# Setup and the first pass of a GNN chain in one block, fourteen sets of one-hot rows with a signal per seven blocks, and running sums in PSUM

## What is computed

```python
edge_index = jnp.stack([src, dst])
x = _layernorm(x + _L0_gnn_ref(x, edge_index, L0_gnn_W1, L0_gnn_b1, L0_gnn_W2, L0_gnn_b2), axis=-1)
x = _layernorm(x + _L1_gnn_ref(x, edge_index, edge_attr_16, L1_gnn_Wf, L1_gnn_bf, L1_gnn_Ws, L1_gnn_bs, ...), axis=-1)
x = _layernorm(x + _L2_gnn_ref(x, edge_index, edge_attr_16, L2_gnn_W, L2_gnn_W_edge, ...), axis=-1)
x = _layernorm(x + _L3_gnn_ref(x, edge_index, batch0, L3_gnn_W1, L3_gnn_b1, ..., L3_gnn_Wf, L3_gnn_bf), axis=-1)
```

```python
def gcn_layer(x, src, dst, W, b, n_nodes):
    h = x @ W
    deg = jax.ops.segment_sum(jnp.ones(src.shape[0], x.dtype), dst, num_segments=n_nodes) + 1.0
    dis = jax.lax.rsqrt(deg)
    norm = dis[src] * dis[dst]
    msg = h[src] * norm[:, None]
    agg = jax.ops.segment_sum(msg, dst, num_segments=n_nodes)
    agg = agg + h * (dis * dis)[:, None]
    return agg + b
```

## Time and profile before

| | us |
|---|---|
| median of 3 runs | 12125.48 |
| lowest, highest | 12105.85, 12148.87 |
| profiled execution, own time | 12032.11 |
| its span | 12030.4 |

### The profile page before, as it was taken

One profiled execution on the slowest core, in us unless ns is written; L12 is line 12 of the kernel. 1 busy time (PEld: TensorE's weight loads), 2 busy tenths in 40 slices (PEclk: granted clock), 3 DMA queues, 4 the chain that ended last, 5 costly groups with the idle time before them and its releaser, 6 DMA issues. The chain is left out here.

```text
span 12030.4 us, 142319 instructions
## 1 busy us (share of the span) xinstructions
PE 6638.5 (55%) x32436; PEld 5450.5 (45%) x32436; DVE 8099.9 (67%) x33889; ACT 5912.3 (49%) x13869; POOL 7313.3 (61%) x6801
## 2 busy tenths in 40 slices
PE   2140666665666466677746666674455465553333
PEld 1020665654555466667745565673233343332221
DVE  2063778995666799989988888444556566764444
ACT  0000445775766799989957776231123332322222
POOL 5700446886777688866636665555654565556665
PEclk6575888887878655568867877555567655665555
DMA  3338777884222477744424444453334333332221
GB/s 95 94 105 268 241 240 253 289 290 154 72 71 71 140 234 236 234 134 142 142 87 160 165 163 146 128 143 84 85 111 129 105 102 90 119 97 56 56 56 52
DMA packets 1019501, 1694.48 MB, mean 141 GB/s; under 512 B 304877, under 2 KB 535080, under 8 KB 1018594
## 3 DMA queue, kind: packets, MB, share of 16 engines
q1 hardware_dynamic: 782752, 1361.06, 33.9%
q0 software_dynamic: 175936, 218.82, 8.4%
q10 hardware_dynamic: 59970, 105.49, 2.7%
HBM read 988.03 MB, written 707.78 MB: 141 GB/s over the span
## 5 line engine op out<-in xcount | busy, mean ns | idle before, releaser
L1319 POOL DMA_INDIRECT g_got<-scaled,row_src x2352 | 2225.1, 946 | 1567.3 <-issue 681.3
L589 PE MATMUL g_a_p_z<-sb_L_gnn_W,g_a_u_t 128*128 128x128 f32 (+3 forms) x2574 | 653.3, 398 | 986.2 <-ACT g_a_u_t L1164 368.0
L881 DVE SCALAR_TENSOR_TENSOR g_sums<-g_got,first,g_sums 128x128 f32<-128x128 f32 (+3 forms) x3136 | 864.2, 276 | 373.6 <-DMA g_got<-scaled,row_src 117.3
L589 PEld LDWEIGHTS g_a_p_z<-sb_L_gnn_W,g_a_u_t 128*128 128x128 f32 (+1 forms) x2574 | 485.0, 267 | 1158.1 <-issue 555.0
L885 DVE SCALAR_TENSOR_TENSOR g_sums<-g_sums,cont,g_got 128x128 f32<-128x128 f32 (+3 forms) x3128 | 880.1, 281 | 125.7 <-DVE g_sums L881 73.1
L1319 POOL DMA_INDIRECT g_got<-xs,idx_src x392 | 369.8, 943 | 926.7 <-POOLq L175 551.1
L1164 ACT COPY g_a_u_t<-g_a_p_t 128x512 f32<-128x512 f32 (+3 forms) x495 | 225.0, 455 | 1393.3 <-remote 762.0
L589 PE MATMUL g_bb_p_z<-sb_L_gnn_W,g_bb_u_t 128*128 128x128 f32 (+2 forms) x4302 | 834.5, 362 | 117.8 <-DVE g_bb_z L1056 76.2
L589 PEld LDWEIGHTS g_bb_p_z<-sb_L_gnn_W,g_bb_u_t 128*128 128x128 f32 x4302 | 754.2, 261 | 165.8 <-issue 137.1
L1164 ACT COPY g_bb_u_t<-g_bb_p_t 128x1024 f32<-128x1024 f32 (+2 forms) x294 | 233.6, 795 | 1123.0 <-PE g_bb_p_t L580 623.7
L1231 POOL DMA_INDIRECT out<-g_a_o,idx_out x396 | 394.5, 996 | 363.1 <-ACT g_a_o L641 250.7
(11 more groups left out here) (495 smaller groups left out, 23885.1 us busy)
## 6 DMA issues: line engine op xcount, KB each, us to landing
raw<-gb_u SPq DMA_DIRECT2D x98, 768.0 KB
xs<-f_o ACTq DMA_DIRECT2D x97, 516.0 KB
f_x<-in_x ACTq DMA_DIRECT2D x97, 512.0 KB
g_bb_own<-in_x SPq DMA_DIRECT2D x97, 512.0 KB
wide<-g_bb_o SPq DMA_DIRECT2D x97, 512.0 KB
g_bb_own<-wide SPq DMA_DIRECT2D x97, 512.0 KB
g_bb_res<-in_x SPq DMA_DIRECT2D x97, 512.0 KB
x<-g_bb_o SPq DMA_DIRECT2D x97, 512.0 KB
```

The lines of the kernel that those rows point to most:

```text
L589: last = nc.tensor.matmul(dst_psum[0:p, q * g * width:(q * g + n) * width], turned_tile[0:n * k, q * P:q * P + p], weight[0:n * k, 0:n * w ...
L881: nc.vector.scalar_tensor_tensor(out=self.firsts, in0=new, scalar=first[:, col], in1=self.firsts, op0=ALU.mult, op1=ALU.add).then_inc(run_ ...
L1319: pool.indirect_dma_start(got[b.s4][:, c * row:(c + 1) * row], None, table, bass.IndirectOffsetOnAxis(ap=index[:, b.n * CH + c:b.n * CH + ...
```

## The change

Three edits, with new constants HOT = 14 and COUNTED = 7.

1. Setup's Block and its barrier are gone; its instructions stand in the first pass's Block. POOL: all constants, then a wait on the new semaphore dst_ready, then the gathers. SP: all loads, then the stores of gathered rows, then gate_wa's stores. ACT: the weight loads, then as before, with setup's square root in step 22 of the scale loop's pipeline. DVE: dst's cast, idx_dst (then dst_ready), hi and lo, the count, the positions; all the rest of setup is a generator, prepare(), of which the scale loop issues one piece (59 in all) after each block. PE: count and p_base, then setup's matmuls and weight_steps.
2. 14 sets of one-hot rows instead of 2, whose memory is given to degree, sums and the like afterwards (so the ones and the cast of node now wait for PE's last block too). PE signals hist_used once for seven blocks, and DVE waits once for seven.
3. In the gated edge pass RunSums uses PSUM: one bank of 512 for the run (one slot), p_c is the first 128 columns of p_d.

```diff
@@ setup's own block goes; what the first pass's block begins with (new, and prepare() cut) @@
-            with nc.Block() as block:
-                @block.gpsimd
...
+                        pool.wait_ge(dst_ready, 1)
...
+                        nc.vector.tensor_scalar(idx_dst[:, :], dst_col[:, :], 0.0, None, ALU.max).then_inc(dst_ready, 1)
...
+                            dve.wait_ge(act_step, 2)
+                            done(nc.vector.reciprocal(inv[:, :], deg_col[:, :]))
+                            yield
...
@@ hot rows and their signal @@
-                hot_hi = [sb(f"hot_hi{s}", [P, CH * 2 * HI], BF16) for s in range(2)]
-                hot_lo = [sb(f"hot_lo{s}", [P, CH * half], BF16) for s in range(2)]
+                with ExitStack() as counting:
+                    hot_hi = [counting.enter_context(nc.sbuf_tensor(f"f_hot_hi{s}", [P, CH * 2 * HI], BF16)) for s in range(HOT)]
+                    hot_lo = [counting.enter_context(nc.sbuf_tensor(f"f_hot_lo{s}", [P, CH * half], BF16)) for s in range(HOT)]
...
-                            if b.after(2):
-                                dve.wait_ge(hist_used, b.n - 1)
+                            if b.after(HOT) and b.n % COUNTED == 0:
+                                dve.wait_ge(hist_used, (b.n - HOT) // COUNTED + 1)
...
-                        nc.vector.memset(ones[:, :], 1.0)
-                        done(nc.vector.tensor_copy(node[:, :], node_i[:, :]))
-                        dve.wait_ge(hist_used, NBE)
+                        dve.wait_ge(hist_used, -(-NBE // COUNTED))
+                        nc.vector.memset(ones[:, :], 1.0)
+                        done(nc.vector.tensor_copy(node[:, :], node_i[:, :]))
...
-                            ins.then_inc(hist_used, 1)
+                            if b.tail or b.n % COUNTED == COUNTED - 1:
+                                ins.then_inc(hist_used, 1)
@@ the scale loop @@
-                        pipeline(dve, [(scale, 0, NB)])
+                        pieces = prepare()
+                        pipeline(dve, [(scale, 0, NB), (lambda b: next(pieces, None), 0, NB)])
+                        for _ in pieces:
+                            pass
...
-                        pipeline(act, [(load, 0, NB), (store, 1, NB)])
+                        def column_roots(b):
+                            act.wait_ge(columns_ready, 5)
+                            nc.scalar.activation(deg_col[:, :], deg_col[:, :], ACT.Sqrt).then_inc(act_step, 1)
+
+                        pipeline(act, [(load, 0, NB), (store, 1, NB), (column_roots, 22, 1)])
@@ RunSums @@
-            def __init__(self, sb, ps, k, tiles, row=None, banked=True):
+            def __init__(self, sb, ps, k, tiles, row=None, p_c=None):
                 self.k, self.row, self.tiles = k, row or k, tiles
-                self.slots = 1 if banked and CH * k == 512 else 2
+                self.slots = 1 if CH * k == 512 else 2
...
+                self.bank, self.taken = ps("sums", [P, 512 if p_c is not None else 1024]), 0
+                self.run = [self.more(CH * k) for _ in range(self.slots)]
+                if p_c is not None:
+                    self.firsts, self.p_c = sb("firsts", [P, k])[:, :], p_c
+                else:
                     self.firsts, self.p_c = self.more(k), self.more(k)
-                else:
-                    self.run = [sb(f"run{s}", [P, CH * k])[:, :] for s in range(self.slots)]
-                    self.firsts, self.p_c = sb("firsts", [P, k])[:, :], ps("p_c", [P, k])[:, :]
...
-                edges = RunSums(sb, ps, D, msg, banked=False)
...
+                edges = RunSums(sb, ps, D, msg, p_c=p_d[:, 0:D])
```

More of the change, by code:

```diff
@@ L18 @@
 UNROLL = 4
+HOT, COUNTED = 14, 7
 LO = 1024
@@ L702, in _, with fill @@
                     def _(sp):
+                        def fill(tile, first_col, table, ready):
+                            sp.dma_start(tile[0:full_p, first_col:first_col + T],
+                                         table[0:full_p * T].rearrange("(p t) -> p t", t=T)).then_inc(ready, DMA)
+                            sp.dma_start(tile[full_p:full_p + 1, first_col:first_col + left_e],
+                                         table[full_p * T:E].rearrange("(p t) -> p t", p=1)).then_inc(ready, DMA)
@@ L709, in _ @@
                             sp.wait_ge(own_stored[s], blocks_in(NBA, s, UNROLL) * DMA)
+                        sp.wait_ge(weight_ready, 1)
+                        with nc.allow_non_contiguous_dma(reason="weights, once"):
+                            for c in range(CH):
+                                sp.dma_start(gate_wa[16 * c:16 * c + 16, c * GW:(c + 1) * GW], gate_w[2][0:16, :]
+                                             ).then_inc(setup_stored, DMA)
+                                sp.dma_start(gate_wa[CH * 16:CH * 16 + 1, c * GW:(c + 1) * GW], gate_w[2][16:17, :]
+                                             ).then_inc(setup_stored, DMA)
@@ L717, in done @@
                             dve.wait_ge(step.sem, step.count())
+                        nc.vector.memset(zeros[:, :], 0.0).then_inc(masked, 1)
+                        nc.vector.memset(eps[:, :], EPS)
+                        nc.vector.memset(gate_wa[:, :], 0.0)
+                        for t in gate_w:
+                            nc.vector.memset(t[:, 2 * D:GW], 0.0)
+                        done(nc.vector.memset(one_t[:, :], 1.0))
+                        dve.wait_ge(index_stored, 4 * DMA)
@@ L858, in more @@
                 self.taken += n
-                assert self.taken <= 1024
+                assert self.taken <= self.bank.shape[1]
                 return self.bank[:, self.taken - n:self.taken]
```

554 lines of the change are left out of this document (271 added, 283 removed).

## The result

| | us |
|---|---|
| after, median of 4 runs | 11683.85 (11659.15 to 11697.76) |
| before, median of 4 runs | 12136.56 (12105.85 to 12148.87) |
| ratio | 0.9629, 95% interval 0.9616 to 0.9642 |
| after, profiled execution, span | 11674.7 |

The change takes 453 us off, where 78 were forecast. The sign was right; the time lies far under the range.

A forecast was written before the change was run, and what follows sets the result against it. Back-to-back gathers were taken to delay PE's completions and starve the first pass's count, followed by a DMA-bound scale loop. -72.8 + 1.6 + 3 - 10 = -78 us gave a 12047 us median, range 11940 to 12115.

The forecast's parts named there:

- The merge: Setup and count joined in the first pass: first gather near 20.6 us, 55 us earlier, hi and lo by 22.0.
- Gathers keep their 528 us: First pass: the 396 gathers take 528 us as before beside the count, ending at 548.6 us.
- the brake: Beside back-to-back indirect DMAs, PE's completions reach other engines in order, one PE instruction per 1.3 to 1.4 us.
- Fourteen sets: Count in first pass: 42 blocks by 570 us, DVE ends at 688.7 instead of 761.5; gain 72.8 us.
- After the count: Rest of first pass: positions chain and 348 us scale loop stay; +1.6 for ones and node cast, +3 for pieces.
- the +1.6: After the count: ones and node cast now stand behind the wait for PE's last blocks, costing 1.6 us.
- The pieces: Scale loop: about 42 us of DVE setup work in 59 pieces, mostly covered, +3 us; +42 if cover fails.
- The gated pass: Gated edge pass with running sums in PSUM: shorter gathers, -10 us, with -69 and +20 as ends.
- (a): Count: the brake is per signal, 22.4 us each, so fewer signals free the count; -300, 11825 us; 12%.
- (b): Count: a longer line is slower still, DVE gets only its first 14 blocks while braked; 12080 us; 10%.
- (c): First pass: pieces not covered (+39), line drains slowly (+19); -20, 12105 us, no measurable change; 8%.
- (d): Gated pass: faster gathers close gaps between bursts, one more group a cycle is braked; +69, 12195 us; 6%.

The follow-up runs named there:

- series A: Runs on a chip where no PE signal is late: kernel before 10416.4 us; changed kernel with 2 sets and a signal per block 10365.67 us.
- series B: Another session, kernel before 12148.2 us: changed kernel as it is 11658.5 us; with 2 sets and a signal per block 12088.85 us.
- the pair of series B: Changed kernel as it is, 11658.5 us, beside the same with 2 sets and a signal per block, 12088.85 us.
- the PSUM run: Changed kernel (14 sets, a signal per seven blocks) with DVE reading its line tables from PSUM: 12056.26 us, kernel before 12049 us.
- the pair: Kernel before, 12042.37 us, beside itself with only the gated pass's running sums in PSUM, 12041.45 us; gated pass 1210.6 and 1209.9 us.

## Why the prediction was wrong, point by point

- **The merge:** right. First gather at 20.80 us (forecast 20.6), hot rows from 22.1 (22.0); with two sets 51 and 59 us under the kernel before in series A and B (55). The wait for SP's first stores, taken as nothing, is 6.6 us in series B's trace with two sets (`DMA xa<-f_got`); it came with one pause of POOL and did not hold the count.
- **Gathers keep their 528 us:** wrong, and this is the step that failed: the forecast let POOL's gathers run on undisturbed beside fourteen sets of rows, and the brake with them. I read the pitch beside DVE's first blocks as "no wait of the size of a hot row", from rows where DVE worked for 3.5 us and then paused. Beside dense rows the pitch is 1.77 us; the gathers take 584 us. By the Trainium skill (SBUF — State Buffer, the box on the "DVE blocks DMA" trap) a DVE instruction in a two-port mode keeps GpSimd from writing descriptors. The traces agree as far as they go: a gather takes 1.47 us instead of 0.95 beside the rows, and the pitch stays 1.25 us where DVE reads its tables from PSUM; the port itself no trace shows. I priced that rule as a loss (30 us) and did not ask what else hangs on POOL's stream.
- **Fourteen sets:** the step "it has passed 7 blocks at 87.3 us, and 7 more every 156.8 us" carried the brake over to a kernel in which DVE does not pause. Measured: DVE never waits for a signal, and the last hot row ends near 196 us instead of 689. This is the mis-sized term of the sum. The form of the brake was right (1.39 us per PE instruction in the PSUM run, against 1.40), its condition was not: it needs gathers at or near their full rate. The 453 us are the merge's 55 and, by the pair of series B, some 400 for this step, where I had 18.
- **After the count:** the ones start 0.3 us after PE's last block, so the +1.6 stands. The scale loop was said to stay at 348 us; it takes some 445, from 240 to 685 us, since it now runs beside the gathers at a DMA share of 0.96. The pieces are covered (forecast +3): with two sets in series B, where no gather runs beside the loop, DVE's part of the loop is 344 us long with the pieces, as it was without them.
- **The gated pass:** forecast -10, measured -0.7 in the pair, one run each, which is nothing. Over all profiles with the sums in PSUM and late signals it takes 1204 to 1223 us without a gap.
- **The rivals:** (a) came nearest in time (11825 us, still 141 us too long), but its mechanism is refuted: 112 instructions with one signal took 156 us. (b) and (c) are out by the times, (d) by the gated pass: no longer with this edit alone.
- By the rule of the Trainium skill on the price of an increment (TensorE: Matmul & The Clock Gate, "The cost: per-tile semaphore tail") 84 signals fewer are worth some 2 us, an estimate. No run resolves that: with 98 signals the kernel took 11565.03 us and with 14 signals 11579.85 on the same chip, one run each.

## What to carry to other kernels

A wait that sits beside back-to-back indirect gathers may be the gathers' doing: give POOL a short pause, or another engine that holds it, before making buffers deeper, and look whether the wait was "remote". And when a rule says that two engines hold each other off, ask what the held engine does to third parties; here its being held was worth 400 us. A pause of POOL is no gain everywhere: g2 became 27 us longer by it and the gated pass 89. A rate measured while an engine pauses does not carry over to a kernel in which it does not.

## What the runs showed that I had not expected

- The same program takes 10416 us on one chip and 12011 to 12148 on others, all of it in passes where PE's signals meet gathers (with the merge and two sets, g3 517 us against 704, first pass 677 against 1093). What sets such a chip apart, or whether it is the chip at all, these runs do not tell.
- The brake: one PE instruction per 1.39 to 1.40 us, in order, at a gather pitch of 1.25 to 1.40 us; gone at 1.44 in the last pass and halved in g5, back in part at 1.34. In the PSUM run DVE's own rows are held to the same 1.40 us, so it is not PE's alone. What carries PE's completions and what POOL does to it stays open; that DVE's or POOL's own accesses loosen the stream is shown, the path is not. A pace that counts instructions, signalling or not, could also come from the recording of each instruction: every run here comes with a recorded span and granted clock, so none here excludes that.
- Two directions of the same hold-off: DVE's rows stretch a gather from 0.95 to 1.47 us, and POOL's clears stretch DVE's rows from 0.27 to 1.70 us.
